# Turned modes laid out by image and mode weights applied after the transposes, in a convolution-attention kernel on one core

## What is computed

```python
def _spectral_conv(x, w2, oh, ow):
    w = w2[..., 0] + 1j * w2[..., 1]
    mh = w.shape[2] // 2
    mw = w.shape[3]
    X = jnp.fft.rfft2(x, norm='forward')
    Xk = jnp.concatenate([X[:, :, :mh, :mw], X[:, :, -mh:, :mw]], axis=2)
    Yk = jnp.einsum('bixy,ioxy->boxy', Xk, w)
...
    return jnp.fft.irfft2(out, s=(oh, ow), norm='forward')
def _fno_layer(x, conv_w, skip_w, oh, ow, inner_norm=False, act=False):
    skip = jnp.einsum('bixy,oi->boxy', x, skip_w)
...
    xf = _spectral_conv(x, conv_w, oh, ow)
    if inner_norm:
        xf = _inorm(xf)
    y = xf + skip
    if act:
        y = jax.nn.gelu(y, approximate=False)
    return y
...
p = _fno_layer(av, Pcw, Psw, H, W)
a = _inorm(p + xa, attn_w, attn_b)
an = _inorm(a, norm2_w, norm2_b)
m = _fno_layer(an, m0cw, m0sw, H, W, inner_norm=True, act=True)
m = _fno_layer(m, m1cw, m1sw, H, W, inner_norm=True, act=False)
out = _inorm(m, mon_w, mon_b) + a
```

## Time and profile before

| | |
|---|---|
| median of three runs | 2213.52 us (2212.35 to 2218.34) |
| profiled execution | 2215.56 us, span 2213.8 us |
| PE busy | 1772.8 us (80%) |
| DVE busy | 1586.3 us (72%) |
| ACT busy | 1097.3 us (50%) |
| POOL busy | 333.1 us (15%) |
| mean granted clock of PE | 0.899 of full |
| end of the part that the diff touches | about 930 us |

### The profile page before, as it was taken

The page is one execution under the profiler, slowest core; times in us unless marked ns, Lnnn a source line. Parts: engine busy times, 40 slices in busy tenths (PEclk is TensorE's granted clock), DMA queues, the critical chain, the costliest instruction groups (busy, mean ns, idle before and its releaser), DMA issues.

```text
span 2213.8 us, 30514 instructions
## 1 busy us (share of the span) xinstructions
PE 1772.8 (80%) x11462; PEld 1128.2 (51%) x11462; DVE 1586.3 (72%) x2741; ACT 1097.3 (50%) x1636; POOL 333.1 (15%) x424
## 2 busy tenths in 40 slices
PE   8865565599775975706999999999999999975856
PEld 8830111199775975603544444445444554443625
DVE  4379999936835426896888788878886888658545
ACT  4286000023544723354676667776777676775110
POOL 0000000000002004571620053103501121110000
PEclk9886777899897997857999999999999999988988
DMA  6450778300010012200000000000000000030396
GB/s 162 186 138 10 175 162 191 91 1 1 1 40 1 1 40 72 87 3 1 1 1 1 1 1 1 1 1 1 1 1 1 1 1 1 1 114 1 136 323 188
DMA packets 95056, 118.42 MB, mean 53 GB/s; under 512 B 15680, under 2 KB 68288, under 8 KB 94112
## 3 DMA queue, kind: packets, MB, share of 16 engines
q1 hardware_dynamic: 94912, 116.46, 18.5%
HBM read 103.99 MB, written 12.44 MB: 53 GB/s over the span
## 4 chain that ended last, share of the span: by engine, by line
PE 63%; DVE 21%; issue 5%; ACT 4%; DMA 3%; POOL 2%; SPq 1%; POOLq 0%; DVEq 0%; ACTq 0%
DVE U L936 7%; PE PS L412 5%; PE PS L414 5%; PE PS L413 5%; PE PS L431 5%; PE PS L433 4%; PE PS L432 4%; PE PS L1152 4%; PE PS L1119 4%; PE PS L1161 4%; PE PS L394 4%; DVE U L968 3%; PE PS L1262 3%; DMA V<-in_L_ffn_weight 2%; PE PS L1131 2%
## 5 line engine op out<-in xcount | busy, mean ns | idle before, releaser
L781 DVE TENSOR_TENSOR DB<-Z 128x1024 f16<-128x1024 f32 (+2 forms) x288 | 337.0, 1170 | 128.8 <-ACT Z L618 76.5
L615 ACT ACTIVATE Z<-PS,MI 128x1024 f32<-128x1024 f32 (+2 forms) x288 | 300.4, 1043 | 229.7 <-PE PS L414 194.4
L767 DVE TENSOR_REDUCE MI<-PS 128x1 f32<-128x512 f32 (+2 forms) x576 | 359.4, 640 | 53.5 <-PE PS L394 34.0
L618 ACT ACTIVATE Z<-PS,MI 128x1024 f16<-128x1024 f32 (+2 forms) x288 | 298.7, 1037 | 0.0
L936 DVE TENSOR_TENSOR U<-A,U 128x4224 f32<-128x4224 f32 x48 | 215.0, 4551 | 0.0
L1249 PE MATMUL PS<-U 128*32 128x352 f32 x1152 | 131.8, 606 | 91.9 <-DVE U L936 91.9
L583 POOL TENSOR_SCALAR Z<-Z,MI 128x128 f32<-128x128 f32 x128 | 86.1, 683 | 718.8 <-DVE MI L796 718.8
L1249 PEld LDWEIGHTS PS<-U 128*32 128x32 f32 x1152 | 39.6, 131 | 183.0 <-DVE U L936 119.4
L949 POOL TENSOR_TENSOR Z<-Z,A 128x704 f32<-128x704 f32 x2 | 6.0, 2980 | 810.4 <-DVE MI L1692 810.4
L1330 ACT ACTIVATE Z<-PS 128x352 f32<-128x352 f32 x6 | 2.8, 463 | 224.0 <-PE PS L1249 224.0
L431 PE MATMUL PS<-Z,A 128*128 128x512 f16 (+3 forms) x288 | 104.1, 361 | 3.9 <-ACT CST L626 3.6
(11 more groups left out here) (408 smaller groups left out, 3879.1 us busy)
## 6 DMA issues: line engine op xcount, KB each, us to landing
V<-in_L_ffn_weight SPq DMA_DIRECT2D x32, 1024.0 KB, 7.5
U<-e_planes SPq DMA_DIRECT2D x192, 132.0 KB, 5.0
A<-x_planes SPq DMA_DIRECT2D x24, 528.0 KB, 10.3
U<-in_x SPq DMA_DIRECT2D x16, 512.0 KB, 3.7
V<-in_x SPq DMA_DIRECT2D x4, 2048.0 KB, 13.8
Z<-in_x SPq DMA_DIRECT2D x16, 512.0 KB, 4.0
out<-U SPq DMA_DIRECT2D x16, 512.0 KB, 5.0
x_planes<-Z SPq DMA_DIRECT2D x2, 1056.0 KB, 8.0
```

The costliest lines, as they stand in the source:

```text
L615: act.activation(EX32[u % 2][:, 0:w], s, ACT.Exp, scale=SCALE / (QUP * KUP), bias=pb).then_inc(sem("ex_ev"), 1)
L618: act.activation(EHI[u % 3][:, 0:w], s, ACT.Exp, scale=SCALE / (QUP * KUP), bias=pb).then_inc(sem("hi_ev"), 1)
L767: dve.tensor_reduce(bm[:, g % 2, t, k:k + 1], PS[:, 4 + chunk_no[c] % 2, 0:w], AX.X, ALU.max).then_inc(sem("ch_ev"), 1)
L781: dve.tensor_tensor(ELO[u % 3][:, 0:w], EX32[u % 2][:, 0:w], EHI[u % 3][:, 0:w], ALU.subtract).then_inc(sem("lo_ev"), 1)
```

## The change

1. A is laid out by mode (66 x 128 images) instead of by image (128 images x 66). Copies into it become scattered by 128 elements, and the stationary operands of `forward` become contiguous. The turned modes are laid out by image (128 x 66), so the copies of the transposes scatter by 66 elements and the stationaries of the rows become contiguous.
2. In layers 1 and 2 the weights are no longer applied to Z. The transposes put kx aside and (ky, real or imaginary) on partitions, so a weight is one number on each partition for a given kx: a table WR of 128 x 33 complex numbers. ACT multiplies the turned 256 elements by the real weight (DVE in two of the 17 groups), DVE adds the imaginary part with two scalar_tensor_tensor for each kx.
3. The variance comes from 33 matmuls of the real-part product with itself (`squares`), whose diagonal is taken and summed by a matmul with `ones`. It is one number for each image along the free dimension, so it is applied to the row results: four copies of 128 columns with a scale of their own in place of one of 512, by ACT or DVE after `rows_by`.
4. The weight tables are loaded once, behind the value stage's loads on SP, and folded through eight small matmuls ahead of layer 0's transposes.
5. `keep` moves from ACT to POOL, as 128 tensor_scalar after the sources of layer 1 are written.
6. Fifteen semaphores become one counter, `once_dve`, in the order of DVE's program.

```diff
-        A = sb("A", [128, N, 2 * KX])
+        A = sb("A", [128, 2 * KX, N])
...
+        AM = Af.rearrange("p (n c x) -> p c x n", c=2, n=N)
+        turned = Af.rearrange("p (n i) -> p i n", n=N)
...
+        BY_DVE = {g for g in range(NTR) if g % 8 == 7}
+        def rows_by(layer, k):
+            by = lambda l, i: "i1_dve" if i % 5 in ((1, 3) if l == 1 else (2,)) else "i1_sc"
...
+            pool.wait_ge(sem("src_ready"), NIM // 2)
+            pool.wait_ge(sem("src_odd"), NIM // 2)
+            for i in range(N):
+                ins = pool.tensor_scalar(U[:, i, :], U[:, i, :], WS[:, 4, i:i + 1], WS[:, 5, i:i + 1], ALU.mult, ALU.add)
+            ins.then_inc(sem("a_kept"), 1)
...
-                        pe.matmul(o, A[:, :, ky], cst["fwr"], start=True, stop=False)
-                        mm = pe.matmul(o, A[:, :, KX + ky], cst["fwi"], start=False, stop=True)
+                        pe.matmul(o, A[:, ky, :], cst["fwr"], start=True, stop=False)
+                        mm = pe.matmul(o, A[:, KX + ky, :], cst["fwi"], start=False, stop=True)
...
+            def weighted_modes(layer):
+                pe.wait_ge(sem("z_ready"), layer + 1)
+                def squares(g):
+                    pe.wait_ge(sem("am_ev"), NTR * (layer - 1) + g + 1)
+                    for x in range(2 * g, min(2 * g + 2, KX)):
+                        mm = pe.matmul(PS[:, 4, 0:128], AM[:, 0, x, :], AM[:, 0, x, :] if x else dc_part, start=x == 0, stop=x == KX - 1)
+                    return mm
+                for g in range(NTR):
+                    if g >= 4:
+                        pe.wait_ge(sem("am_ev"), NTR * (layer - 1) + g - 3)
+                    for x in range(2 * g, min(2 * g + 2, KX)):
+                        for c in range(2):
+                            mm = pe.matmul(PS[:, g % 4, 256 * (x % 2) + 128 * c:256 * (x % 2) + 128 * c + 128], Zk[:, c:c + 2, :, x], ident,
+                                           is_transpose=True, start=True, stop=True)
+                    mm.then_inc(sem("tr_mm"), 1)
+                    if g >= 3:
+                        squares(g - 3)
...
+                pe.wait_ge(sem("dg_ready"), layer)
+                pe.matmul(PS[:, 6, 0:128], ones, image_diag, start=True, stop=True).then_inc(sem("once_mm"), 1)
...
+            pe.wait_ge(sem("wf_ready"), 1)
+            for i in range(2):
+                for c in range(2):
+                    for h in range(2):
+                        mm = pe.matmul(PS[KY * h:KY * h + KY, 5, 2 * i + c:2 * i + c + 1], wrow[:, i, :, c], ident[0:1, 0:1], start=True, stop=True)
...
-                dve.tensor_copy(A[:, 4 * k:4 * k + 4, :].rearrange("p n k -> p (n k)"), PS[:, k % 4, 0:264]).then_inc(sem("f1_ev"), 1)
+                dve.tensor_copy(A[:, :, 4 * k:4 * k + 4].rearrange("p k n -> p n k"), PS[:, k % 4, 0:264].rearrange("p (n k) -> p n k", n=4)).then_inc(sem("f1_ev"), 1)
...
+                            ins = act.activation(AM[:, :, x, :], PS[:, g % 4, 256 * (x % 2):256 * (x % 2) + 256].rearrange("p (c n) -> p c n", c=2),
+                                                 ACT.Copy, scale=WR[:, layer - 1, x, 0:1])
...
+                                ins = act.activation(DB[0:66, k % 3, 128 * j:128 * j + 128], PS[0:66, 4 + k % 2, 128 * j:128 * j + 128],
+                                                     ACT.Copy, scale=image_rstd[0:66, 4 * k + j:4 * k + j + 1])
...
+                dve.tensor_scalar(Z[:, 2, :], Z[:, 0, :], -1.0, None, ALU.mult).then_inc(sem("z_ready"), 1)
+                for x in range(KX):
...
+                    first = dve.scalar_tensor_tensor(AM[:, 0, x, :], t[:, 1], WN[:, layer - 1, x:x + 1], AM[:, 0, x, :], ALU.mult, ALU.add)
...
+                    ins = dve.scalar_tensor_tensor(AM[:, 1, x, :], t[:, 0], WR[:, layer - 1, x, 1:2], AM[:, 1, x, :], ALU.mult, ALU.add)
...
+                dve.tensor_tensor(image_diag, PS[:, 4, 0:128], ident, ALU.mult).then_inc(sem("dg_ready"), 1)
...
+                dve.reciprocal(image_rstd, image_var).then_inc(sem("rs_ready"), 1)
```

More of the change, by code:

```diff
@@ L270, in conv_attn_hybrid @@
         NF2, NTR, NIM = 11, 17, 32
+        BY_DVE = {g for g in range(NTR) if g % 8 == 7}
+        def rows_by(layer, k):
+            by = lambda l, i: "i1_dve" if i % 5 in ((1, 3) if l == 1 else (2,)) else "i1_sc"
+            mine = by(layer, k)
+            return mine, sum(by(l, i) == mine for l in range(1, layer + 1) for i in range(NIM if l < layer else k + 1))
         NU = UB * B
@@ L1156, in columns @@
                 def columns(k):
[L1157 removed]
+                    rows_out(k)
                     if k >= 2:
@@ L1336, in inverse_evacs @@
             def inverse_evacs(layer):
[L1337 removed]
+                for g in range(1, NTR, 2) if layer == 0 else ():
                     act.wait_ge(sem("tr_mm"), layer * NTR + g + 1)
[L1339 to L1344 removed]
+                    act.activation(turned[:, 4 * g:4 * g + 4, :], PS[:, g % 4, :].rearrange("p (i n) -> p i n", i=4), ACT.Copy).then_inc(sem("tr_ev1"), 1)
@@ L1363, in _ @@
                 ins.then_inc(sem("src_odd"), 1)
-            def keep(images):
-                for i in range(images.start, images.stop):
-                    ins = act.activation(U[:, i, :], U[:, i, :], ACT.Identity, scale=WS[:, 4, i:i + 1], bias=WS[:, 5, i:i + 1])
-                ins.then_inc(sem("a_kept"), 1)
-            act.wait_ge(sem("src_ready"), NIM // 2)
-            keep(slice(0, 24))
             for layer in (1, 2):
@@ L1708, in _ @@
-                later(dve.tensor_scalar(lay[:, 2:3], lay[:, 2:3], 2.0, EPS, ALU.mult, ALU.add))
-                dve.scalar_tensor_tensor(lay[:, 2:3], lay[:, 3:4], -1.5, lay[:, 2:3], ALU.mult, ALU.add).then_inc(sem("var_ready"), 1)
-                dve.wait_ge(sem("root_ready"), 4 + layer)
-                dve.reciprocal(lay[:, 6:7], lay[:, 2:3]).then_inc(sem("rstd_ready"), 1)
-                dve.wait_ge(sem("rstd_ready"), layer)
-                later(dve.tensor_scalar(Z[:, 0, :], Z[:, 2, :], lay[:, 6:7], None, ALU.mult))
@@ L1714, in _ @@
-                dve.wait_ge(sem("z1_scaled"), layer)
-                dve.tensor_scalar(Z[:, 2, :], Z[:, 0, :], -1.0, None, ALU.mult).then_inc(sem("z_ready"), 1)
-                transposed_evacs(layer)
-                sw = PAR["m0sw"] if layer == 1 else PAR["m1sw"]
-                for k in range(NIM):
-                    dve.wait_ge(sem("i2_mm"), NIM * layer + k + 1)
-                    v4 = Vn[:, 4 * k:4 * k + 4, :]
-                    y = dve.scalar_tensor_tensor(v4, v4, sw, PS[:, 6 + k % 2, :].rearrange("p (n w) -> p n w", w=W), ALU.mult, ALU.add)
+                all_emptied(dve, "f2_ev", layer + 1, NF2)
@@ new lines, in _ @@
+                dve.tensor_scalar(Z[:, 2, :], Z[:, 0, :], -1.0, None, ALU.mult).then_inc(sem("z_ready"), 1)
+                for x in range(KX):
+                    t = PS[:, x // 2 % 4, 256 * (x % 2):256 * (x % 2) + 256].rearrange("p (c n) -> p c n", c=2)
+                    if x // 2 in BY_DVE:
+                        dve.wait_ge(sem("tr_mm"), layer * NTR + x // 2 + 1)
+                        later(dve.tensor_scalar(AM[:, :, x, :], t, WR[:, layer - 1, x, 0:1], None, ALU.mult))
+                    else:
+                        dve.wait_ge(sem("am_act"), (NTR - len(BY_DVE)) * (layer - 1) + sum(g not in BY_DVE for g in range(x // 2 + 1)))
+                    first = dve.scalar_tensor_tensor(AM[:, 0, x, :], t[:, 1], WN[:, layer - 1, x:x + 1], AM[:, 0, x, :], ALU.mult, ALU.add)
+                    if x == 0:
+                        later(first)
+                        dve.tensor_scalar(dc_part, AM[:, 0, 0, :], 0.25, None, ALU.mult)
+                    ins = dve.scalar_tensor_tensor(AM[:, 1, x, :], t[:, 0], WR[:, layer - 1, x, 1:2], AM[:, 1, x, :], ALU.mult, ALU.add)
+                    if x % 2 or x == KX - 1:
+                        ins.then_inc(sem("am_ev"), 1)
@@ new lines, in _ @@
+                dve.wait_ge(sem("rs_ready"), layer)
+                sw = PAR["m0sw"] if layer == 1 else PAR["m1sw"]
+                for k in range(NIM + 1):
+                    if k < NIM and rows_by(layer, k)[0] == "i1_dve":
+                        dve.wait_ge(sem("i1_mm"), NIM * layer + k + 1)
+                        if k >= 3:
+                            dve.wait_ge(sem("i2_mm"), NIM * layer + k - 2)
+                        for j in range(4):
+                            ins = dve.tensor_scalar(DB[0:66, k % 3, 128 * j:128 * j + 128], PS[0:66, 4 + k % 2, 128 * j:128 * j + 128],
+                                                    image_rstd[0:66, 4 * k + j:4 * k + j + 1], None, ALU.mult)
+                        ins.then_inc(sem("i1_dve"), 1)
+                    if k == 0:
+                        continue
+                    dve.wait_ge(sem("i2_mm"), NIM * layer + k)
+                    v4 = Vn[:, 4 * k - 4:4 * k, :]
+                    y = dve.scalar_tensor_tensor(v4, v4, sw, PS[:, 6 + (k - 1) % 2, :].rearrange("p (n w) -> p n w", w=W), ALU.mult, ALU.add)
```

209 lines of the change are left out of this document (106 added, 103 removed).

## The result

The changed kernel takes 2145.84 us (median of three runs, 2144.72 to 2150.56) against 2213.52: ratio 0.9694, 95% interval 0.9663 to 0.9726. The profiled execution has 2145.84 us too, span 2144.1; granted clock 0.909.

What follows compares the result with a forecast made beforehand. It took `forward` to be PE-bound by its strided stationary, with PE idle between forward and rows. Terms of -50.7, +5.5, -11.0, -12.3, +3.7, +0.8, -1.4, +1.6, +0.7 gave -63.1: 2151 us, range 2138 to 2182.

Steps and rivals of the forecast that it cites:

- What bounds the kernel: `forward`, three layers: PE-bound, the stationary's step costing more than half; contiguous A saves 3 x 16.9 = 50.7 us.
- The copies that write A turned: Layer 1's first step: scattered copies lengthen DVE's turn from 1.82 to 2.16 us, 16 turns, +5.5; other layers 0.
- Between `forward` and rows: Last forward copy to first row matmul, layers 1 and 2: 33.5 us after, saving 11.0 and 12.3.
- T: Pipeline of 17 groups between negation and tail, layers 1 and 2: DVE 27.5 plus filling and draining, 30 us.
- tail: After the 17 groups: diagonal, matmul, variance, root, reciprocal and first scaled copy, minus two row groups; 2.1 us net.
- draining: End of the 17-group pipeline; with filling (first transposes, first ACT group) it adds 2.5 us to DVE's 27.5.
- `keep` on POOL: Keeping `a`: 128 x 0.683 = 87 us on POOL, hidden under layers 1 and 2; 0.3 us carried for the negation.
- Rows scaled by image: Row results: four copies take 1.15 us on ACT, 1.12 on DVE; layer 1 +3.7, layer 2 +0.8.
- Small: Fold matmuls ahead of layer 0's transposes +1.6 us; those transposes, bound by strided copies, +0.7; weight loads 0.
- Rival (a): Squares' moving operand pays too; if costs add, 0.49 us an instruction, +26 over two layers, 2177 us; chance 0.13.
- Rival (c): The stationary's step isn't the cause; `forward` stays at 0.245 us, the sum loses 50.7, 2202 us; chance 0.05.
- (d): Weighted transposes run hand over hand without overlap: 4.7 us a group, 80 us for 17 groups, 2251 us; chance 0.03.

Runs made afterwards that it cites:

- A by image: The changed kernel with A alone laid out by image again, its copies and scaling included; 2202.79 us, 0.9930 against the kernel before.
- only A by mode: The kernel before with A alone laid out by mode (shape, copies, scaling, `forward`'s operands); 2167.86 us, ratio 0.9775.
- Squares of constants: The changed kernel with the squares multiplying the identity matrix by itself after the same waits; 2145.81 us, one run.

## Why the prediction was right, and where it was off

- *What bounds the kernel.* Right. To the first matmul behind layer 2 the A by image kernel gives back 46.7 us and the only A by mode kernel takes 51.3; -49.4 measured for three `forward`s against -50.7. Layer 0 gains 2 us less than the others, since its window's clock is 0.88: its first 17 contiguous instructions take 0.22 us each at half clock, where the strided ones before took 0.243 at either level.
- *The copies that write A turned.* This is the term that was mis-sized: +5.5 predicted for layer 1's first step, +0.8 measured. The duration was right (0.60 expected, 0.614), but I put 1.14 us for two copies in DVE's turn. The timeline of DVE in the changed kernel:

```profile
577.14 1.07 DVE L1506 COPY A<-PS 128x264 f32<-128x264 f32 x2
578.05 1.09 DVE L1724 TENSOR_SCALAR V<-U,MI 128x128 f32<-128x128 f32 x4
579.06 1.06 DVE L1506 COPY A<-PS 128x264 f32<-128x264 f32 x2
```

  The next instruction starts 0.91 us after the first of two copies, 0.455 each; the remaining 0.16 of each lies under the next. The turn is 0.91 + 1.01 = 1.92 against 1.82, and 16 x 0.1 = 1.6. The +0.8 of the account is this less a luckier clock (0.95 for 0.92 before); at one clock it was 1.7 to 2.0. The earlier trace rows already showed the same overlap (0.80 for two copies of 0.43), and I added the whole lengthening on top of it.
- *Between `forward` and rows.* Right, -22.3 against -23.3, and for the reason given: DVE's chain, four products a group 0.36 apart, 27.5 us predicted and 26.9 from first start to last start measured. Squares of constants leave T at 31.4. The prediction's T, without its tail, is 30.6 (622.3 to 652.9) against 30; the wait of 1.56 us was in its draining, the half clock behind it was not in the sum. One reading was off without harm: 9.78 / 66 = 0.148 for a transpose mixes two clock levels, 0.213 at half clock and 0.123 at full.
- *`keep` on POOL.* Hidden, as said. It takes 56 us, not 87: 0.45 each but for one. The mean of the row I used, L583, mixes some 110 instructions of 0.60 with 17 of 1.1 to 1.5; why its short ones are dearer than 0.45 isn't shown. The 0.3 us that I carried for DVE's negation waiting for POOL didn't come: it takes 1.27 us beside POOL in layer 1 and 1.26 without it in layer 2. It was POOL that stood: its instruction that starts at 621.06, 0.06 us after the negation, takes 1.53. DVE's products are as quick beside it in layer 1 as without it in layer 2 (T 31.54 and 31.35).
- *Rows scaled by image.* Four copies take 1.13 on ACT and 1.12 on DVE, 1.15 and 1.12 predicted; +2.7 and +0.1 against +3.7 and +0.8.
- *Small.* The fold is 0.64 us of PE and adds 0.6, a third of the guess. Layer 0's transposed copies take 1.12 and 1.14 for 1.02, +0.6.
- *Rival (a)* rested on load and moving stream adding. They don't (the squares' instructions start 0.243 us apart, strided twice). Its other half, that the moving operand's step costs at all, is true, which I had left open. *Rival (c)* fell with the A by image kernel, (d) with 17 groups 1.44 us apart.
- *Not seen at all:* that the by-image layout of the turned modes loses about 15 us. I costed the change only as a whole against the kernel before. Everything for it was in the sum: a scattered write on DVE, ACT and a strided read on PE in every group, against 0.05 us a turn for the rows, which layer 0 (1.5 us) and layer 2 (1.1) could use and layer 1 not.
- *Luck.* The total, -67.7 us of the median against -63.1, is made of terms that missed both ways: +5.5 for the copies is 3.5 to 4.7 too dear, and the half clock behind PE's wait, some 1.6 us in layer 1, was in no term.

## What to carry to other kernels

A layout has a writer and a reader on each side: price every access that it makes strided, part by part, and try the part that only moves the stride around on its own; here one of two layouts gained about 50 us and the other lost about 15, and the sum hid it. In a chain of overlapping instructions take the distance between starts, not the duration, and carry the overlap over to the changed form. Where PE waits for the last item of another engine's chain, the wait can also halve its clock for what follows. And before a microsecond is put down to an edit, compare the granted clock of the two stretches.

## What the runs showed of the hardware

- A 32-bit matmul of 128 moving columns is two instructions. They start 0.112 us apart with contiguous operands, 0.118 with a step of 8 bytes in the stationary, and 0.22 to 0.245 with 16 bytes or more in the stationary or 128 or more in the moving operand; both strided cost no more than one. 512 moving columns cover it, 66 stationary columns nearly do (0.125).
- The transposes (L1147 after) are one instruction each, and their stationary steps by 132 bytes. They start 0.123 us apart at full clock and 0.213 at half, so the price above is not theirs; why isn't shown.
- At the 1.2 GHz level contiguous instructions of such a matmul take 0.213 to 0.22 us and strided ones 0.243, as at full clock: the strided operand's pace is set by something that the granted clock doesn't slow.
- Products on DVE (scalar_tensor_tensor, 128 columns, one input in PSUM), with the other input and the output at a step of 264 bytes in SBUF: 0.36 us apart for 0.26 contiguous. ACT's 256 elements, output at that step: 0.731 for 0.475.
